# Fused LoRA, cross-attention and graph kernel: the softmax sums are laid out over all value rows by TensorE's sum products, and the products that handed out their inverses are dropped

## The reference

```
scores = jnp.where(mask, scores, -jnp.inf)
attn = jax.nn.softmax(scores, axis=-1)
ctx = jnp.einsum('bhlv,bvhd->blhd', attn, Vv).reshape(B, L, H)
attn_out = ctx @ Wo.T + bo
```

## Time and profile before

| | before |
|---|---|
| median of 3 runs | 455.51 us (455.42 to 456.22) |
| the profiled execution: time | 458.76 us |
| the profiled execution: span from first to last instruction | 457.0 us |
| PE busy | 404.4 us (88%) |
| DVE busy | 287.7 us (63%) |
| ACT / POOL busy | 142.5 / 138.3 us |
| mean granted TensorE clock | 0.944 of full speed |

### The profile page before, as it was taken

The page is one execution under the profiler, slowest core; times in us unless marked ns, Lnnn a source line. Parts: engine busy times, 40 slices in busy tenths (PEclk is TensorE's granted clock), DMA queues, the critical chain, the costliest instruction groups (busy, mean ns, idle before and its releaser), DMA issues.

```text
span 457.0 us, 6017 instructions
## 1 busy us (share of the span) xinstructions
PE 404.4 (88%) x2376; PEld 321.8 (70%) x2376; DVE 287.7 (63%) x331; ACT 142.5 (31%) x165; POOL 138.3 (30%) x95
## 2 busy tenths in 40 slices
PE   4978497699898879976879989999999999999996
PEld 1664467465746655756537688898988988898894
DVE  1899647656687586787364676656556564565733
ACT  2230051405134422543171333242333124223310
POOL 2273532007104430360010243423434243244400
PEclk9979797979799889989979999999999999999999
DMA  7920452106210623054000000000000000000022
GB/s 197 407 76 1 161 126 53 47 23 138 42 46 24 130 51 93 1 113 65 1 0 1 0 1 0 1 1 1 0 0 0 1 0 0 0 0 0 1 80 104
DMA packets 20357, 22.73 MB, mean 50 GB/s; under 512 B 4304, under 2 KB 15440, under 8 KB 20336
## 3 DMA queue, kind: packets, MB, share of 16 engines
q1 hardware_dynamic: 19312, 21.26, 16.6%
q0 software_dynamic: 576, 1.18, 1.3%
q10 hardware_dynamic: 448, 0.01, 0.1%
HBM read 12.74 MB, written 3.15 MB: 35 GB/s over the span
## 4 chain that ended last, share of the span: by engine, by line
PE 72%; DVE 15%; issue 6%; ACT 5%; DMA 1%; POOL 1%; SPq 0%; DVEq 0%; ACTq 0%
PE slot L469 69%; DVE shift L1238 3%; ACT probT L809 1%; PE slot L579 1%; DVE x L1197 1%; DVE mix L1167 1%; DMA xyz_n<-in_ctx 1%; DVE x L1194 1%; DVE x_in L1183 1%; ACT adj L848 1%; DVE p_lo L1112 1%; DVE inv_sums L1038 1%; DVE near_of L1029 1%; DVE points L1059 1%; PE slot L628 1%
## 5 line engine op out<-in xcount | busy, mean ns | idle before, releaser
L903 POOL TENSOR_TENSOR p_lo<-p_full,p_hi 128x1024 fp32r<-128x1024 f32 x29 | 69.5, 2399 | 159.1 <-ACT p_hi L687 159.1
L687 ACT ACTIVATE p_hi<-p_full 128x1024 fp32r<-128x1024 f32 x32 | 33.9, 1060 | 127.1 <-DVE p_full L987 127.0
L1076 DVE TENSOR_TENSOR u_lo<-slot,u_hi 128x1024 fp32r<-128x1024 f32 x32 | 38.9, 1225 | 53.2 <-ACT u_hi L725 53.2
L469 PE MATMUL slot<-adj,u_hi 128*128 128x512 f32 x256 | 65.0, 396 | 0.2
L469 PE MATMUL slot<-adj,u_lo 128*128 128x512 f32 x256 | 63.3, 389 | 0.0
L1083 DVE SCALAR_TENSOR_TENSOR points<-slot,points 128x1024 f32<-128x1024 f32 x32 | 39.2, 1224 | 33.8 <-PE slot L469 33.8
L469 PE MATMUL slot<-fs_hi,p_hi 128*128 (+1 forms) x256 | 51.7, 284 | 6.7 <-DVE p_lo L1112 4.4
L469 PEld LDWEIGHTS slot<-adj,u_lo 128*128 128x128 f32 x256 | 48.1, 188 | 10.1
L469 PEld LDWEIGHTS slot<-adj,u_hi 128*128 128x128 f32 x256 | 46.5, 188 | 10.5 <-issue 1.8
L469 PE MATMUL slot<-fs_hi,p_lo 128*128 (+1 forms) x256 | 51.6, 283 | 0.0
L469 PE MATMUL slot<-fs_lo,p_hi 128*128 (+1 forms) x256 | 51.5, 283 | 0.0
(11 more groups left out here) (143 smaller groups left out, 574.5 us busy)
## 6 DMA issues: line engine op xcount, KB each, us to landing
q_stack<-q_hi SPq DMA_DIRECT2D x32, 128.0 KB, 2.5
x_in<-in_xT SPq DMA_DIRECT2D x4, 512.0 KB, 3.8
q_stack<-q_lo SPq DMA_DIRECT2D x16, 128.0 KB, 5.0
out_points<-points SPq DMA_DIRECT2D x4, 512.0 KB, 2.8
loraB_raw<-in_lora_BT SPq DMA_DIRECT2D x1, 1024.0 KB, 9.7
wk<-in_WkT SPq DMA_DIRECT2D x1, 1024.0 KB, 11.7
wq_raw<-in_WqT SPq DMA_DIRECT2D x1, 1024.0 KB, 10.7
wv<-in_WvT SPq DMA_DIRECT2D x1, 1024.0 KB, 12.5
```

The source lines that it names most:

```text
L469: return pe.matmul(dst, lhsT, rhs, start=start, stop=stop, skip_group_check=True)
L687: act.activation(p_hi[:, b, :], p_full[:, half, :], ACT.Copy).then_inc(p_hi_ready, 1)
L903: pool.tensor_tensor(lo, full, hi.bitcast(F32), ALU.subtract).then_inc(ready, 1)
L1076: dve.tensor_tensor(u_lo[:, half].rearrange("p m o -> p (m o)"), ps[:], u_hi[:, half].rearrange("p m o -> p (m o)").bitcast(F32), ALU.subt ...
```

## The change

`sum_cols` becomes one 128x32 matrix of two blocks of ones: the sum product now gives every one of the 32 value rows of a head pair a copy of its head's sum. Each "attend" tile writes 256 columns of its own (start and stop), so "sums" fills a 128x1024 slot. DVE inverts all of it into a wider `inv_sums`, and multiplies at once `attT` with `inv_sums`, both in SBUF. The list entry "norm", its products, `row_of` and its construction on POOL are gone. Cut to its core:

```diff
@@ tile_order
-                  ("distance", n, 1), ("attend", b, 2), ("attend", b, 3), ("query", n, 0), ("norm", b, 0)]
+                  ("distance", n, 1), ("attend", b, 2), ("attend", b, 3), ("query", n, 0)]
...
-              ("norm", b, 0), ("spread", 1, 0), ("output", b, 0), ("spread", 2, 0),
+              ("spread", 1, 0), ("output", b, 0), ("spread", 2, 0),
@@ buffers
-        inv_sums = fb("inv_sums", [P, S])
-        sum_cols = fb("sum_cols", [P, KC, PART])
-        row_of = fb("row_of", [P, KC, P])
+        inv_sums = fb("inv_sums", [P, KC, S])
+        sum_cols = fb("sum_cols", [P, PART])
@@ PE, attend
                     for j in range(4):
-                        last = mm(slot(("sums", b, 0))[PART * j:PART * (j + 1), 0:S], sum_cols[:, i, :],
-                                  probT[:, i % 2, j * S:(j + 1) * S], i == 0, i == KC - 1)
+                        last = mm(slot(("sums", b, 0))[PART * j:PART * (j + 1), i * S:(i + 1) * S], sum_cols[:],
+                                  probT[:, i % 2, j * S:(j + 1) * S], True, True)
@@ PE, norm
-                elif kind == "norm":
-                    pe.wait_ge(inv_ready, b + 1)
-                    for c in range(KC):
-                        last = mm(ps[:, c * S:(c + 1) * S], row_of[:, c, :], inv_sums[:], True, True)
@@ POOL, mixed
-                    link(pool.memset(row_of[:], 0.0))
-                    for c in range(KC):
...
-                    last.then_inc(vblk_consts, 1)
@@ DVE
             def invert(b):
 
                 wait_attend(dve, b, KC - 1)
-                if b >= 1:
-
-                    wait_full(dve, "norm", b - 1, 0)
-                dve.reciprocal(inv_sums[:], slot(("sums", b, 0))[:, 0:S]).then_inc(inv_ready, 1)
-
-            def divide(b, ps):
+                dve.reciprocal(inv_sums[:].rearrange("p c s -> p (c s)"), slot(("sums", b, 0))[:]).then_inc(inv_ready, 1)
+
+            def divide(b):
 
 
                 dve.wait_ge(att_read, b + 1)
-                wait_full(dve, "norm", b, 0)
-                dve.tensor_tensor(attT[:].rearrange("p c s -> p (c s)"), attT[:].rearrange("p c s -> p (c s)"), ps[:],
-                                  ALU.mult).then_inc(att_ready, 1)
+                dve.wait_ge(inv_ready, b + 1)
+                dve.tensor_tensor(attT[:], attT[:], inv_sums[:], ALU.mult).then_inc(att_ready, 1)
...
                 elif kind == "attend" and i == KC - 1:
+                    if b >= 1:
+                        dve.wait_ge(att_ready, b)
                     invert(b)
-                elif kind == "norm":
-                    divide(b, ps)
+                    divide(b)
```

More of the change, by code:

```diff
@@ L159, in xattn_graph_kernel @@
         v_blk = fb("v_blk", [P, NH // 2, PART])
-        inv_sums = fb("inv_sums", [P, S])
-        sum_cols = fb("sum_cols", [P, KC, PART])
-        row_of = fb("row_of", [P, KC, P])
-        fb("room_v", [P, 640])
+        inv_sums = fb("inv_sums", [P, KC, S])
+        sum_cols = fb("sum_cols", [P, PART])
+        fb("room_v", [P, 480])
         wq_raw, = under(("wq_raw", [P, KC, H], F32))
@@ L330, in xattn_graph_kernel @@
             "sums": (inv_ready, lambda b, i: b + 1), "attend": (att_read, lambda b, i: b + 1),
-            "norm": (att_ready, lambda b, i: b + 1),
             "adjacency": (adj_ready, lambda b, i: b + 1), "output": (sum_ready, lambda b, i: ST * (b + 1)),
@@ L607, in _ @@
                     pe.wait_ge(vblk_ready, 2 * (b + 1))
-                    pe.wait_ge(vblk_consts, 2)
-                    pe.wait_ge(dve_consts, 13)
+                    pe.wait_ge(vblk_consts, 1)
+                    pe.wait_ge(dve_consts, 7)
                     pe.wait_ge(prob_ready, KC * b + i + 1)
@@ L1208, in _ @@
                         dve.wait_ge(dve_consts, 5)
[L1209 to L1212, removed]
+                        for half in range(2):
+                            dve.memset(sum_cols[half * V:(half + 1) * V, half * HD:(half + 1) * HD], 1.0)\
+                               .then_inc(dve_consts, 1)
                         dve.wait_ge(k_stack_zero, 1)
```

## The result

The changed kernel takes **463.69 us** (median of 4 runs, 462.41 to 464.40), the kernel before 455.87 us on the same chip (4 runs, 455.42 to 456.79). The ratio is 1.0166, with a 95% interval of 1.0134 to 1.0198: slower by 1.7%. The forecast of 458.4 us had the sign; its range ended at 461.0, 2.7 us too low. Some executions of a program fall into a slower state: the ratios leave these out, the medians given here include them, the profiled execution of e7 was such a one, and that of e6, which ran once, may be.

What follows compares the result with a forecast made beforehand. The prediction took PE to bound the kernel (72% of the span on the last chain, DVE 15%). Its terms, -0.5 - 0.5 + 2.0 + 3.1 + 0.3 - 1.5 = +2.9 us, added to the 455.51 median, gave 458.4 us, range 455.9 to 461.0.

Steps and rivals of the forecast that it cites:

- batch 0: Behind batch 0's attention: "query" covers the longer inversion, "adjacency" waits for it, PE keeps 0.5 of 1.7 us: -0.5 us.
- my rivals: Clock costs nothing (456.1 us, 14%); faster (454.4, 6%); clock costs its bound (461.5, 12%); reciprocal longer than its line (465.8, 4%).
- three signs of being wrong: Reciprocal leaving its line, batch 2's addition not delayed, or the clock staying at the upper level in batch 1.
- Batch 1: Behind batch 1's attention: "lora_a" waits for the inversion, -0.5 us at equal clock, plus 2.0 us of lower clock after PE idles.
- term of 2.0: Batch 1, from "lora_a" to the end of "square": lower clock after 4.8 us of PE idleness costs +2.0 us.
- my two bounds: Batch 1's clock cost: nothing if the clock stays up, 3.4 us if the lower level lasts and all of it is work.
- Batch 2: Behind batch 2's attention, DVE is the path: the longer inversion delays the second `p_lo`, +3.1 us, plus +0.3 of clock.
- Batch 3: Behind batch 3's attention, PE is the path: it drops "norm", so "spread" and "output" start earlier: -1.5 us.
- The sum: Whole kernel: the batch and clock terms add to +2.9 us, giving 458.4 us, 0.6% slower.

Runs made afterwards that it cites:

- e7: Changed kernel, inverting only the first 256 of 1,024 columns and multiplying with these, so three quarters of the inverses are left out: 458.19 us, ratio 1.000 to before.
- e6: Changed kernel with a 128x300 memset on POOL ahead of the key blocks of batches 1 to 3: 470.59 us, one execution.
- e2: The changed kernel run again, unchanged, for a second profile: 464.50 us, ratio 1.0153 to the kernel before.
- e3: Changed kernel with POOL's key blocks of batches 1 to 3 waiting until DVE has written `mix`, behind `lgw`: 463.28 us, ratio 1.0133 to before.
- e10: Changed kernel with the key blocks held back from `lgw`, repeated with 12 runs: 457.93 us, ratio 1.0020 to before.
- e15: Changed kernel with one 128x480 memset on POOL ahead of the `k_stack` DMA issues: 463.58 us, one execution.
- e16: Changed kernel with two 128x480 memsets on POOL ahead of the `k_stack` DMA issues: 460.00 us, one execution.
- e1: The kernel before run again, unchanged, for a second profile: 457.76 us, one run.
- e4: Kernel before with POOL's key blocks of batches 1 to 3 waiting until DVE has written `mix`: 456.63 us, ratio 0.9972 to before.
- e11: Changed kernel with key blocks held back and the inversion in two halves, the first behind the second "attend" tile: 452.59 us, ratio 0.9923 to before.
- e12: Changed kernel with key blocks held back and only 256 of 1,024 columns inverted, three quarters of the inverses left out: 449.22 us, ratio 0.9817 to before.

## Why the prediction was wrong, point by point

**The step that failed** is batch 0: "DVE loses nothing, the cover is the "query" product on PE", and from it "**-0.5 us**". Up to "adjacency" it held: the changed kernel's rows of PE behind batch 0 read

```profile
101.75 1.07 PE L622 MATMUL slot<-ident_wide,near_of 128*128 128x128 bf16 x16 [1.07 <-DVE inv_sums L1023]
102.66 1.90 PE L467 MATMUL slot<-x_in,a_router 128*72 128x256 f32 x8
```

"adjacency" is released by `inv_sums` 6.60 us behind the inversion's start, where I had put 6.66. But I followed only PE and DVE from there, and took the stretch's end to move with them; POOL stood in no term. Counted from the inversion's start, `lgw` began at 13.50 us instead of 14.06, since PE was ahead, and POOL ended its issues at 13.57 instead of 13.37, since `q_lo` took longer (2.62 us for 2.36, in e2 2.59, where the product of `attT` from SBUF lies beside it). The key blocks, which before had a pause of 0.39 us for PE, now followed the issues at once; `lgw` fell into the last issue and waited for all four. The measured term is +3.5 us; without the stall it is 47.6 to 49.0 (e3, e10, e15, e16) against 48.4 to 49.9 (before, e1, e4), in which -0.5 fits. (One kernel repeats there only to 1.1 us: e3 and e10 have 48.73 and 47.59.) None of my rivals was this one: they had clocks and the reciprocal, no second engine beside a DVE operation of 0.17 us. None of its three signs of being wrong showed: the reciprocal kept its line, batch 2's addition was delayed, and the clock fell in batch 1.

**Batch 1** (+1.5 forecast, +1.0 measured) went as described. In the changed kernel, PE:

```profile
149.44 1.06 PE L622 MATMUL slot<-ident_wide,near_of 128*128 128x128 bf16 x16
154.98 3.43 PE L467 MATMUL slot<-x_in,a_router 128*72 128x256 f32 x8 [4.48 <-DVE inv_sums L1023]
158.06 1.28 PE L467 MATMUL slot<-k_blk_hi,q_hi 128*128 128x512 f32 x4
159.51 1.04 PE L467 MATMUL slot<-xyz_sq,half_neg 64*65 64x512 f32 x2 [0.17 <-issue]
```

PE idles 4.48 us (forecast: over 4). "lora_a" then takes 3.43 us for 1.90, and "scores" and "square" are back at full speed. The clock costs 1.5 us for a term of 2.0, between my two bounds; how much it costs varies, in e16 it was 1.0 us more in "scores" alone. The windows of the changed kernel around it (length, busy us of PE, PEld, DVE, ACT, POOL, granted clock, DMA):

```profile
149.20:153.60 4.40, 1.30 (x20) 1.11 (x18) 4.40 (x1) 3.30 (x4) 2.76 (x2) 1.00 0.29 66
153.90:157.30 3.40, 2.32 (x6) 1.41 (x7) 3.30 (x3) 0.00 (x0) 2.59 (x5) 0.60 0.89 208
```

The granted clock still reads 1.00 while PE idles and 0.60 in the stretch behind it; the forecast said 0.50. In e11 and e12, with 1.28 us of idleness or none, "lora_a" took 1.95 and 1.90 us.

**Batch 2** (+3.1 and +0.3 of clock; +2.9 measured). DVE runs without a pause from the inversion to the second `p_lo`, as forecast:

```profile
197.18 6.54 DVE L1023 RECIPROCAL inv_sums<-slot 128x1024 f32<-128x1024 f32 x1
203.83 1.23 DVE L1030 TENSOR_TENSOR attT<-attT,inv_sums 128x1024 f32<-128x1024 f32 x1
204.97 2.28 DVE L1270 TENSOR_TENSOR fs_lo<-fs_raw,fs_hi 128x2048 fp32r<-128x2048 f32 x1
207.18 1.22 DVE L1207 TENSOR_TENSOR points<-slot,bo_all 128x1024 f32<-128x1024 f32 x1
...
216.39 1.22 DVE L1096 TENSOR_TENSOR p_lo<-p_full,p_hi 128x1024 fp32r<-128x1024 f32 x1
```

The addition begins 10.00 us behind the inversion's start, 6.23 before: 3.77 more for a forecast of 3.65. The second `p_lo` begins 19.21 behind it, 15.93 before: +3.28 for +3.1.

**Batch 3** (-1.5 forecast, -1.6 measured). In the changed kernel, PE:

```profile
246.88 2.00 PE L467 MATMUL slot<-adj,u_hi 128*128 128x512 f32 x8
...
250.97 7.11 PE L467 MATMUL slot<-wo,attT 128*128 128x512 f32 x16 [0.27 <-issue]
```

"spread" stands directly behind "wp", and "output" begins 7.99 us behind the inversion's start, after the product (ready at 250.9). Before it was 10.56. That is more than the 1.5 us of "norm", but one profile each: in e2 and e1 it begins 8.76 and 12.05 us behind, because "wp" ahead of it starts and runs differently. The stretches of one kernel differ by 0.7 and 1.4 us between its two profiles, so the mechanism is shown, and that -1.6 comes so near to -1.5 is luck.

**The sum.** +2.9 forecast, +5.8 by the stretches: batch 0 adds 4.0, the other three together take 1.1. That explains 2.9 of the 5.3 us between 458.4 and 463.69. Of the rest, 0.4 is that the median before was 455.87 us with the fourth run and 455.51 without, and 2.0 that the medians of the first chip differ by 7.8 us where the stretches add up to 5.8; most of the timed executions have no trace, so I can't place it. The profiled execution before was 2.9 us longer than its median, that of the changed kernel 1.3 us shorter than its own, and the opening alone moves by as much.

**What stays open.** Why `lgw` then lets all four key blocks pass first isn't shown by any row, only that it does, in both kernels; a DMA issue alone doesn't hold it (0.17 us in e3). The wait of 0.6 us in the two cases of the last but one issue, against 0 for the third from last, fits no account of mine either.

## What to carry to other kernels

Price a long DVE operation by the slope of its own rows in the trace: that worked to 0.2%. Then follow *all* engines past the end of the edited place, to the next short DVE operation with two inputs in SBUF that stands beside a run of GpSimd work: a shift of half a microsecond in its arrival can cost a whole run of blocks, and a semaphore that orders the two cost nothing that could be measured here, where the blocks had slack (e4, 0.9972). Trading PE products for a DVE inversion four times as wide paid here only once the inversion was cut up and a part of it put where DVE waits anyway.

## What the runs showed that I had not expected

- A DVE operation of 0.17 us took 4.13 to 4.61 us in five profiles of both kernels, when it began within the last DMA issue of POOL with four blocks of 1.01 us ready behind; 0.72 to 1.04 us when it began 0.03 to 0.36 us into the first block. In that case it always ended 1.07 to 1.10 us behind the block's start, and so waited for that one block only.
- The opening, nearly the same work up to the first inversion, took 94.1 to 99.8 us in fourteen profiles, and 103.6 in e6 and e7. Cutting at markers inside the execution gave stretches that repeat to 0.2 us in two of the four for the first two profiles of each kernel (49.67 and 49.87, 53.23 and 53.26; 47.79 twice, 48.80 and 48.86), but the other two differ by 0.7 to 1.4 us, and e3 and e10, one kernel, by 1.1 us in the first.
- The stall costs more than itself: PE idles 4.3 to 4.8 us behind it, and its next eight transposes take 0.9 us more at the lower level of the clock. `lgw` is 4.0 us longer, and the stretch from inversion 0 to 1 was 4.3 to 5.7 us longer in the changed kernel (53.2 us, against 48.96 in e15, 48.73 in e3, 47.59 in e10 and 47.55 in e16).
